# Two-layer decoder block on one core: the group pipeline of the first layer put in another order

## The chip, the core and the metric

The kernel runs on one core of a Trainium2 chip. The core has five engines that run their own instruction streams and meet at semaphores: TensorE (PE, with its weight loads PEld), VectorE (DVE), ScalarE (ACT), GpSimd (POOL) and SyncE (SP), which here only issues DMAs. The metric is the device time of one execution in microseconds (us).

## The reference, cut to what matters

A batch of 16 sequences of 100 tokens, 256 wide, goes through two decoder layers. Each is x + self-attention, then x + cross-attention to a context of 361 rows, then x + a mixture of experts. The change touches the first layer up to its experts. Cut to its core, this is:

```python
# A: attention over random features
h = layernorm(x)
q = tanh(h @ W_charge.T + b);  shell = h @ W_shell.T + b;  shell /= norm(shell)
proj = shell @ omega.T + rff_bias
phi_s = concat([cos(proj), sin(proj)]);  phi = (powers_of(q) x phi_s) @ W_combine.T
logits = phi @ phi.T * T / temp          # causal mask, softmax
x = x + (softmax(logits) @ V) @ W_out.T + b_out
# B: cross-attention
h = layernorm(x)
x = x + softmax(q(h) @ k(ctx).T) @ v(ctx)
# C: block with 16 causal heads of 16; D: router and experts
h = layernorm(x, ln1);   x1 = h + ...     # the normed x enters the sum
x = x + attention(h) @ wo + bo
scores = layernorm(x, ln2) @ gate_w      # top 2 of 8 experts, softmax over the two
```

## The kernel before, in words

The 16 sequences are four groups of four (`NB = 4`, `NG = 4`), and each group is two halves h of two sequences (200 tokens). In the first layer two kinds of work are laid side by side:

- `early(g, h)` takes half h of group g through A and B. It is one chain of small steps: norm (`norm_dve`), transpose (`turn_pe`, `turn_act`), the product `A_in` (L933), square and norm of the shell (L1901 to L1908), the angle (`A_omega`, L943, then six DVE instructions L1913 to L1923, named the angle chain here), the sine on ACT (L1440), the product `A_comb` (L947), nine DVE instructions L1930 to L1938 (the phi chain), the logits, softmax, values, `A_out`; then B with its own softmax. The last step of B adds to `x` and writes `xall`.
- `behind(g, routed)` takes the whole group g through C, the layer's attention with 16 heads (`attend`, 19 steps of which 16 make scores), and D, the router's scores. If `routed`, it also does the routing of the group before: `route` on DVE in two parts (ranking; then places, after `ahead`, L1026 to L1029, has counted tokens on PE), and eight indirect DMAs `send` on POOL.

`in_turn(early(0, 0), early(0, 1))` runs first, alone. Then `woven` is called for each group g from 0 to 2: it deals out `ROUNDS` rounds, in each one step of early(g+1, 0), one of behind(g), one of early(g+1, 1), one of behind(g). The yields of the generators are the steps; every engine has its own copy of them. The call for g = 0 stands alone, those for 1 and 2 are a loop (`Fori`). At the end behind(3) runs alone. What counts for the order: each engine does its instructions strictly in the order that this dealing gives, so an instruction that waits holds up everything dealt after it, on its engine, of both kinds of work.

In `attend`, step n makes scores n on PE (L1041, L1044) in one of two PSUM banks; DVE takes the maximum (L1995), subtracts (L1999); ACT takes the exponential (L1489); PE transposes (L1052), ACT copies (L1495), PE multiplies by the values (L1063); DVE sums (L2005). POOL builds `headbd` (L1708) for two steps ahead. `root_pool` (L466 ff.) does the inverse root of a norm on POOL.

The softmax quotient of A (L1954, L1956) and B (L1977, L1980) is multiplied into the exponentials before they are transposed.

## Time and profile before

| | us |
|---|---|
| median of three runs | 1689.74 (1689.53 to 1692.46) |
| the profiled execution's own time | 1689.45 |
| its span, first to last instruction | 1687.8 |
| PE busy / DVE / ACT / POOL | 1285.4 / 998.3 / 522.3 / 415.1 |

The span divides into: preparation to 20 us; early(0) alone from 21 to 92; the woven groups 0, 1 and 2 from 92 to 215, to 338 and to 464; behind(3) alone to 540; then the experts of the first layer and the whole second layer, which the change doesn't touch. "Idle before" in a row is the time in which the engine stood still ahead of that instruction, and the name behind the arrow is what ended it. The granted clock is the share of TensorE's full clock that it was given.

### The profile page before, as it was taken

How to read it: one execution, taken by the hardware profiler on the slowest of the kernel's cores; microseconds unless marked ns; L12 is line 12 of the kernel's file. 1: busy time of each engine (PE TensorE's matmuls, PEld its weight loads, DVE VectorE, ACT ScalarE, POOL GpSimd, SP SyncE). 2: the span in 40 equal slices, each digit the busy share in tenths (PEclk: the TensorE clock that was granted, in tenths of full speed). 3: DMA queues.
4: the chain of work that ended last, by engine and by line, in shares of the span. 5: the costliest groups of instructions: out<-in, count | busy, mean ns of one | idle time of the engine just before them, and what ended most of it. 6: DMA issues, size and time to landing. Idle time of an engine off the chain costs nothing.

```text
span 1687.8 us, 24678 instructions
## 1 busy us (share of the span) xinstructions
PE 1285.4 (76%) x7936; PEld 890.2 (53%) x7936; DVE 998.3 (59%) x2156; ACT 522.3 (31%) x1279; POOL 415.1 (25%) x528
## 2 busy tenths in 40 slices
PE   2677868767877699981458977779787697986987
PEld 1554654644644366651237754467554475644755
DVE  4447557457455233325676765768656686677852
ACT  2214324324322222210125512346213363233620
POOL 1032143243253200006622111311212212032100
PEclk9778878878888799995679989779897799987988
DMA  9510010191014211101315310044100350104501
GB/s 376 217 28 1 19 28 13 34 408 49 25 46 198 59 47 44 44 29 45 117 39 98 86 40 12 10 101 111 40 12 2 86 122 21 32 11 88 114 5 46
DMA packets 69693, 122.37 MB, mean 73 GB/s; under 512 B 25404, under 2 KB 55100, under 8 KB 68032
## 3 DMA queue, kind: packets, MB, share of 16 engines
q1 hardware_dynamic: 63936, 110.04, 21.7%
q0 software_dynamic: 5632, 10.77, 2.3%
q8 instruction: 66, 1.08, 0.3%
q14 instruction: 59, 0.48, 0.1%
HBM read 67.69 MB, written 53.07 MB: 72 GB/s over the span
## 4 chain that ended last, share of the span: by engine, by line
PE 46%; issue 24%; DVE 12%; POOL 8%; DVEq 3%; ACT 3%; DMA 2%; POOLq 2%; SPq 0%; ACTq 0%
PE ps L1143 7%; PE ps L1390 5%; PE ps L1162 3%; PE ps L525 3%; PE ps L1316 3%; PE ps L1332 3%; PE ps L533 2%; POOL experts L1779 2%; PE ps L1302 2%; PE ps L1403 2%; PE ps L933 1%; PE ps L1041 1%; POOL headbd L681 1%; PE ps L504 1%; DVE probs L1999 1%
## 5 line engine op out<-in xcount | busy, mean ns | idle before, releaser
L1628 ACT ACTIVATE probs<-ps,small 100x361 f32<-100x361 f32 x256 | 141.3, 557 | 94.1 <-DVE small L2347 89.5
L2347 DVE TENSOR_REDUCE small<-ps 100x2 f32<-100x722 f32 x128 | 115.7, 906 | 36.2 <-PE ps L1302 36.2
L1143 PE MATMUL ps<-every,xT_t 128*128 x256 | 122.3, 601 | 0.4 <-issue 0.4
L1390 PE MATMUL ps<-hT,experts 128*128 128x400 f32 x288 | 117.1, 558 | 1.2 <-DVE small L730 1.2
L1316 PE MATMUL ps<-cst,probs 100*121 100x100 f32 x768 | 104.0, 271 | 8.1 <-DVE probsT L2355 7.7
L1316 PEld LDWEIGHTS ps<-cst,probs 100*121 100x121 f32 x768 | 94.8, 185 | 22.2 <-issue 13.7
L2355 DVE TENSOR_SCALAR probsT<-ps 121x600 f32<-121x600 f32 x128 | 99.2, 775 | 9.1 <-PE ps L1316 9.1
L1332 PE MATMUL ps<-probsT,values_ 121*32 121x100 f32 x1536 | 90.8, 253 | 0.9 <-DVE probsT L2355 0.9
L1302 PE MATMUL ps<-k_stack,q_stack 96*100 96x362 f32 x256 | 81.8, 400 | 6.3 <-ACT probs L1628 5.6
L473 POOL TENSOR_TENSOR small<-small,cst 100x2 f32<-100x2 f32 x56 | 11.1, 198 | 295.3 <-DVE small L453 295.2
L1390 PEld LDWEIGHTS ps<-hT,experts 128*128 128x128 f32 x288 | 59.6, 215 | 42.2 <-issue 14.1
L681 POOL TENSOR_TENSOR headbd<-kT,cst 128x800 f32<-128x800 f32 x32 | 48.6, 1525 | 126.1 <-DVE kT L2237 95.7
L1192 PE MATMUL ps<-identb,xq 100*128 100x100 bf16 x128 | 13.4, 240 | 83.9 <-DVE y L2222 46.9
L504 PE MATMUL ps<-cst,xn 100*128 100x100 f32 x192 | 35.1, 328 | 52.3 <-DVE xn L459 34.7
L1403 PE MATMUL ps<-experts,probsT 128*100 128x256 f32 x288 | 70.2, 388 | 4.0 <-DVE probsT L2382 3.5
L594 PE MATMUL ps<-headbd,qT 128*100 128x400 f32 x128 | 60.1, 553 | 13.4 <-POOL headbd L681 13.4
L1332 PEld LDWEIGHTS ps<-probsT,values_ 121*32 121x32 f32 x1536 | 62.4, 109 | 13.9 <-DVE probsT L2355 1.8
L1708 POOL TENSOR_TENSOR headbd<-kT,cst 128x800 f32<-128x800 f32 x32 | 48.9, 1528 | 82.3 <-PE ps L1044 70.0
L1795 POOL TENSOR_TENSOR k_hi<-k_all,cst 128x362 fp32r<-128x362 f32 x32 | 26.4, 824 | 165.0 <-ACT k_all L1580 165.0
L1489 ACT ACTIVATE probs<-probs 100x400 f32<-100x400 f32 x64 | 34.3, 537 | 101.3 <-DVE probs L1999 101.2
L1995 DVE TENSOR_REDUCE small<-ps 100x4 f32<-100x400 f32 x64 | 36.5, 570 | 48.4 <-PE ps L1044 46.5
L1041 PE MATMUL ps<-headbd,qT 128*100 128x400 f32 x128 | 60.7, 558 | 3.2 <-ACT qT L1515 2.6
(329 smaller groups left out, 2887.2 us busy)
## 6 DMA issues: line engine op xcount, KB each, us to landing
k_stack<-key_d SPq DMA_DIRECT2D x192, 90.5 KB, 3.1
tok_d<-wt SPq DMA_DIRECT2D x1, 14848.0 KB, 45.5
res_d<-wt SPq DMA_DIRECT2D x1, 14848.0 KB, 42.0
every<-e_d SPq DMA_DIRECT2D x8, 1536.0 KB, 11.6
ctxT<-ctxT_d SPq DMA_DIRECT2D x8, 726.0 KB, 4.3
key_d<-k_hi SPq DMA_DIRECT2D x32, 181.0 KB, 2.8
key_d<-k_lo SPq DMA_DIRECT2D x32, 181.0 KB, 3.4
gates<-gate_d SPq DMA_DIRECT2D x28, 200.0 KB, 4.4
```

Source lines behind the costliest of these rows:

```text
L594: e.matmul(o, qT[:, c, b * S:(b + 1) * S], headbd[:, u % 2, 4 * i:4 * i + 4, :].rearrange("p h n -> p (h n)"), start=True, stop=False)
L681: inc(e.tensor_tensor(headbd[:, u % 2], keysT[:, c, b * S:(b + 1) * S].unsqueeze(1).broadcast_to([P, HC, S]), cs("head").unsqueeze(2).broa ...
L1041: e.matmul(o, qT[:, c, b * S:(b + 1) * S], headbd[:, m // 2 % 2, 4 * q:4 * q + 4, :].rearrange("p h n -> p (h n)"), start=True, stop=False)
L1143: ins = e.matmul(ps[:, 2 * i + t % 2, :], xT_t[:, t % 2, c, :], every[:, bass.ds(base + (i * DC + c) * HID0, HID0)], start=(c == 0), stop= ...
L1302: ins = e.matmul(bank(2 * (n % 2) + i, S, LE), q_stack[:, c * HC + h, b * S:(b + 1) * S], k_stack[c][:, h // 2, :], start=True, stop=True)
L1316: ins = e.transpose(ps[0:KW, 4 + i, k * S:(k + 1) * S], f_e[:, n % 2, i, k * KW:(k + 1) * KW], identS)
L1332: ins = e.matmul(ps[quarter(h), 6, (2 * (b % 2) + c) * S:(2 * (b % 2) + c + 1) * S], strip(3 * (b % 2) + k, KW, c, h), f_eT[:, n % 2, i, k ...
L1390: ins = e.matmul(bank(2 * i + j % 2, n=NT), w[:, c, :], hT[:, c, :], start=(c == 0), stop=(c == DC - 1))
L1403: ins = e.matmul(ps[0:S, 4 + b // 2, (b % 2) * D:(b % 2 + 1) * D], g_hid[:, (j - 1) % 2, b * S:(b + 1) * S], experts[:, o - D:o], start=(j ...
L1628: ins = e.activation(f_e[:, n % 2, i, 0:LC], bank(2 * (n % 2) + i, S, LC), ACT.Exp, bias=h_nm[:, n % 2, i:i + 1], accum_out=h_sum[:, b, h: ...
L2347: inc(e.tensor_reduce(h_nm[:, n % 2, 0:2], ps[0:S, 2 * (n % 2):2 * (n % 2) + 2, 0:LC], AX, ALU.max, negate=True), "F_nm")
L2355: inc(e.tensor_scalar(f_eT[:, n % 2], ps[0:KW, 4:6, 0:KC * S], 1.0, None, ALU.mult), "F_pT")
```

## The change: what it does

Six things, all in the first layer:

1. A's norm of group g+1 is drawn ahead: its statistics and its scaling are two steps (`norm_ahead`) dealt near the end of the group before, behind B's `B_qbk` and `B_nm` steps on DVE, its roots on POOL likewise. `early` begins with the transpose on PE. Since nothing else then orders them, PE's `A_in` waits for a new signal `B_x`, set by the last step of B.
2. Both parts of `route` and the PE part `ahead` move: part one to behind the scaling of C's norm, part two and `ahead` into attention step 0. PE waits for the places at step 3 rather than at C's second projection. POOL's eight sends go to steps 7, 9, 11, 13, 14, 15, 16 and 17.
3. Empty steps are set behind long chains (after the angle chain, after `A_out`, after B's softmax, and at places in `behind`): `ROUNDS` goes from 18 to 20.
4. One sine instruction for both halves, which waits for the second half's angles.
5. The quotients of A's and B's softmax are left off the exponentials, and the token's reciprocal is multiplied in by the instruction that adds the result to `x` (two `scalar_tensor_tensor` of 100x256 in place of one `tensor_tensor` of 100x512).
6. The loop over groups 1 and 2 is written out.

```diff
-ROUNDS, STEPS = 18, 19
+ROUNDS, STEPS = 20, 19
+SEND_AT = {7: 0, 9: 1, 11: 2, 13: 3, 14: 4, 15: 5, 16: 6, 17: 7}
...
             def early(g, h):                                    # PE
-                yield
                 turn_pe(e, "A_", g, h, "hTp", p, xnX, ("A_xn", 1))
                 yield
                 W(e, "A_hT", g, 1, h)
+                if g:
+                    W(e, "B_x", g - 1, 1, h)
...
                 for n in range(STEPS):                          # PE, attend
                     if n < 16:
                         scores(n)
+                    if routed and n == 0:
+                        ahead(g - 1)
                     if 2 <= n <= 17:
                         turn(n - 2)
+                    if routed and n == 3:
+                        e.wait_ge(r_placed.sem, r_placed.at(g - 1))
...
             in_turn(early(0, 0), early(0, 1))
-            woven(early(1, 0), early(1, 1), behind(0, False))
-            with e.Fori(1, NG - 1) as g:
-                woven(early(g + 1, 0), early(g + 1, 1), behind(g, True))
+            for g in range(NG - 1):
+                woven(early(g + 1, 0), early(g + 1, 1), behind(g, g > 0))
             list(behind(NG - 1, True))
...
-                W(e, "A_ang", g, 1, h)                          # ACT
-                inc(e.activation(a_trig[:, t], a_ang[:, t], ACT.Sin), "A_trig")
+                yield
+                if h == 0:
+                    W(e, "A_ang", g, 1, 1)
+                    e.activation(a_trig, a_ang, ACT.Sin).then_inc(names["A_trig"].sem, 2)
...
+            def norm_ahead(g, h):                               # DVE
+                e.wait_ge(ld["x"].sem, g * 16 + 16)
+                inc((yield from norm_dve(e, "A_", g, h, xin, xnX)), "A_xn")
+                yield
+
             def early(g, h):
                 p, q, t, o = 2 * h, 2 * h + 1, tok(h), own(h)
-
-                if h == 0:
-                    e.wait_ge(ld["x"].sem, g * 16 + 16)
-                inc((yield from norm_dve(e, "A_", g, h, xin, xnX)), "A_xn")
+                norm = norm_ahead(g + 1, h) if g + 1 < NG else iter(())
...
-                W(e, "A_e", g, 1, h)
-                e.reciprocal(a_rs[:, o], a_sum[:, o])
-                e.drain()
-                inc(e.tensor_tensor(lg, lg, a_rs[:, o].unsqueeze(2).broadcast_to([S, HB, S]), ALU.mult), "A_p")
                 yield
                 yield
                 W(e, "A_out", g, 1, h)
                 W(e, "A_xb", g, 1, h)
-                add_out(x, p, h)
+                e.reciprocal(a_rs[:, o], a_sum[:, o])
+                e.drain()
+                for i, b in enumerate(seqs(h)):
+                    e.scalar_tensor_tensor(x[:, b, :], ps[0:S, p, i * D:(i + 1) * D], a_rs[:, b:b + 1], x[:, b, :],
+                                           ALU.mult, ALU.add)
...
                 inc(e.tensor_scalar(b_qbk[:, o], bank(p, S, HB), 1.0, None, ALU.mult), "B_qbk")
+                next(norm, None)
                 yield
...
                 for h in range(2):                              # DVE, behind
                     list(norms[h])
                     e.drain()
                     for b in seqs(h):
                         ins = e.tensor_scalar(xn[:, b, :], y[:, b, :], r2Y[:, b:b + 1], None, ALU.mult)
                     inc(ins, "C_xn")
-                    if h == 0:
-                        next(ways, None)
-                    yield
+                    yield
+                next(ways, None)
+                yield
```

Three places in the order. First DVE, ahead of the attention of groups 1 and 2, before the change: `L1995` and `L1999` are the first attention step's maximum and difference, `L1913` to `L1923` the first half's angle chain.

```order
L1908 TENSOR_TENSOR values_<-values_,small 100x2x64 x2
L426 ISA
L1995 TENSOR_REDUCE small<-ps 100x4
L1999 TENSOR_TENSOR probs<-ps,small 100x400
L1913 TENSOR_SCALAR values_<-ps,wt 64x200
L1915 TENSOR_SCALAR values_<-values_ 64x200
L1917 TENSOR_SCALAR values_<-values_ 64x200
L1919 SCALAR_TENSOR_TENSOR values_<-values_ 64x200
L1921 SCALAR_TENSOR_TENSOR values_<-values_ 64x200
L1923 TENSOR_SCALAR values_<-values_ 64x200
```

The same place after it (lines are shifted: `L1929` to `L1939` is the second half's angle chain, `L2017` and `L2021` the maximum and difference, `L2061` the copy of C's values out of PSUM):

```order
L2061 TENSOR_SCALAR xn<-ps 100x512
L1929 TENSOR_SCALAR values_<-ps,wt 64x200
L1931 TENSOR_SCALAR values_<-values_ 64x200
L1933 TENSOR_SCALAR values_<-values_ 64x200
L1935 SCALAR_TENSOR_TENSOR values_<-values_ 64x200
L1937 SCALAR_TENSOR_TENSOR values_<-values_ 64x200
L1939 TENSOR_SCALAR values_<-values_ 64x200
L2017 TENSOR_REDUCE small<-ps 100x4
L2021 TENSOR_TENSOR probs<-ps,small 100x400
```

Both angle chains now stand ahead of the attention's first step instead of behind its first and second.

What stands on DVE behind that first step in groups 1 and 2 after the change (`L2104` to `L2118` is the routing's second part, `L2110` its wait for PE's count, `L1947` the start of the phi chain):

```order
L2017 TENSOR_REDUCE small<-ps 100x4
L2021 TENSOR_TENSOR probs<-ps,small 100x400
L2104 TENSOR_TENSOR small<-small 100x32
L2106 TENSOR_REDUCE small<-small 100x4
L2108 TENSOR_TENSOR small<-small 100x4
L2110 TENSOR_TENSOR small<-small,ps 100x64
L2113 TENSOR_REDUCE small<-small 100x8
L2114 TENSOR_REDUCE small<-small 100x8
L2116 CAST place_all<-small 100x8
L2117 CAST place_now<-small 100x8
L2118 TENSOR_TENSOR small<-small 100x8
L1947 TENSOR_SCALAR values_<-ps 100x2x64
```

The routing's second part has moved from ahead of C's projections to between the first attention step and the first phi chain.

Then PE, late in the attention of group 0, before: `L533` is the second `A_out` product, `L1041` with `L1044` are scores, `L1052` a transpose, `L1063` values, `L504` the transpose of B's first normed half.

```order
L1052 MATMUL ps<-cst,probs 100x100 x4
L1063 MATMUL ps<-probsT,values_ 32x100 x4
L533 MATMUL ps<-wt,experts 100x256 x4
L1041 MATMUL ps<-headbd,qT 100x400
L1044 MATMUL ps<-causalb,identb 100x400
L1052 MATMUL ps<-cst,probs 100x100 x4
L1063 MATMUL ps<-probsT,values_ 32x100 x4
L504 MATMUL ps<-cst,experts 128x100 x4
L1041 MATMUL ps<-headbd,qT 100x400
```

After (`L1046` and `L1049` scores, `L1057` transpose, `L1068` values, `L505` the transpose of B's first half; the row above the first is the scores product that belongs to it, and the second `A_out` product is directly before that):

```order
L1049 MATMUL ps<-causalb,identb 100x400
L1057 MATMUL ps<-cst,probs 100x100 x4
L1068 MATMUL ps<-probsT,values_ 32x100 x4
L1046 MATMUL ps<-headbd,qT 100x400
L1049 MATMUL ps<-causalb,identb 100x400
L1057 MATMUL ps<-cst,probs 100x100 x4
L1068 MATMUL ps<-probsT,values_ 32x100 x4
L1046 MATMUL ps<-headbd,qT 100x400
L1049 MATMUL ps<-causalb,identb 100x400
L1057 MATMUL ps<-cst,probs 100x100 x4
L1068 MATMUL ps<-probsT,values_ 32x100 x4
L505 MATMUL ps<-cst,experts 128x100 x4
```

Between the second `A_out` and B's first transpose there now stand three whole attention steps instead of one.

## Rows read from the trace of the kernel before

**Rows 1.** Windows by stage; columns: us, busy us (instructions) per engine, granted clock, DMA share

```profile
91.60:214.70 123.10, 91.59 (x533) 63.63 (x532) 73.87 (x180) 41.25 (x96) 34.71 (x46) 0.85 0.06 16
214.70:338.10 123.40, 93.41 (x542) 64.83 (x542) 75.61 (x199) 41.24 (x96) 43.50 (x54) 0.83 0.08 24
...
214.70:247.60 32.90, 20.47 (x94) 16.09 (x94) 19.04 (x60) 5.66 (x14) 15.52 (x25) 0.74 0.08 22
247.60:267.50 19.90, 15.02 (x55) 7.29 (x55) 15.89 (x41) 8.85 (x13) 6.45 (x6) 0.69 0.04 12
267.50:302.80 35.30, 28.45 (x212) 17.97 (x209) 24.81 (x57) 14.66 (x38) 14.50 (x16) 0.98 0.04 12
...
464.10:488.20 24.10, 14.64 (x67) 12.55 (x67) 10.91 (x38) 3.86 (x8) 9.70 (x17) 0.72 0.18 67
```

**Rows 2.** Timeline of PE, opening of a group: start us, us, form [idle before <-releaser]

```profile
220.91 1.15 PE L1029 MATMUL ps<-small,cst 100*100 100x24 f32 x6
...
231.94 3.72 PE L933 MATMUL ps<-wt,experts 128*100 128x321 f32 x8
...
238.58 2.33 PE L933 MATMUL ps<-wt,experts 128*100 128x321 f32 x8
...
247.68 0.91 PE L1041 MATMUL ps<-headbd,qT 128*100 128x400 f32 x2 [0.61 <-ACT qT L1515]
```

**Rows 3.** Timeline of DVE, same group, opening and first attention steps

```profile
217.56 0.19 DVE L2072 TENSOR_REDUCE small<-small 100x4 f32<-100x32 f32 x1
...
220.08 0.26 DVE L2076 TENSOR_SCALAR small<-small 100x32 f32<-100x32 f32 x2
...
230.55 0.61 DVE L2032 TENSOR_SCALAR xn<-y,small 100x256 f32<-100x256 f32 x2
...
250.48 1.55 DVE L1915 TENSOR_SCALAR values_<-values_ 64x200 f32<-64x200 f32 x1
...
255.69 0.26 DVE L1915 TENSOR_SCALAR values_<-values_ 64x200 f32<-64x200 f32 x1
...
259.00 0.28 DVE L1930 TENSOR_SCALAR values_<-ps 100x128 f32<-100x128 f32 x1
...
261.91 0.29 DVE L1938 TENSOR_TENSOR values_<-values_,ps 100x128 f32<-100x128 f32 x1
```

**Rows 4.** Timeline of POOL, same group

```profile
222.82 0.20 POOL L473 TENSOR_TENSOR small<-small,cst 100x2 f32<-100x2 f32 x1 [0.23 <-DVE small L453]
...
225.33 0.71 POOL L484 TENSOR_TENSOR small<-small,cst 100x2 f32<-100x2 f32 x1
...
250.39 1.52 POOL L1708 TENSOR_TENSOR headbd<-kT,cst 128x800 f32<-128x800 f32 x1 [1.63 <-PE ps L1044]
```

**Rows 5.** Timeline of ACT, same group, around the sines

```profile
254.05 1.28 ACT L1489 ACT_TABLE_LOAD   x1
255.34 0.54 ACT L1489 ACTIVATE probs<-probs 100x400 f32<-100x400 f32 x1
```

**Rows 6.** Timeline of PE, same group, middle and end

```profile
280.19 0.38 PE L964 MATMUL ps<-cst,values_ 100*100 100x100 f32 x2 [2.09 <-DVE values_ L1956]
...
283.72 0.38 PE L964 MATMUL ps<-cst,values_ 100*100 100x100 f32 x2 [1.50 <-DVE values_ L1956]
...
301.37 0.56 PE L504 MATMUL ps<-cst,experts 100*128 100x100 f32 x4 [2.69 <-DVE experts L459]
...
326.31 3.17 PE L533 MATMUL ps<-wt,qT 128*100 128x256 f32 x8 [1.99 <-DVE qT L2048]
```

**Rows 7.** Timeline of DVE, same group, end

```profile
331.95 0.74 DVE L459 TENSOR_SCALAR bdx<-y,small 100x256 f32<-100x256 f32 x2 [0.27 <-issue]
```

**Rows 8.** DVE by line and form: count | busy us, mean ns | idle before

```profile
L2296 DVE SCALAR_TENSOR_TENSOR x<-ps,small,xall 100x256 f32<-100x256 f32 x16 | 7.0, 478 | 2.7 <-PE ps L533 1.8 <-issue 0.8
...
L1986 DVE TENSOR_TENSOR xall<-ps,x 100x512 f32<-100x512 f32 x4 | 2.8, 692 | 11.2 <-PE ps L1017 11.2
```

**Rows 9.** Timeline of PE, front of the first group, nothing beside it

```profile
40.13 4.71 PE L947 MATMUL ps<-wt,values_ 64*100 64x320 f32 x8 [2.11 <-ACT values_ L1440]
```

More of the change, by code:

```diff
@@ L1525, in behind @@
                     yield
[L1526 to L1527 removed]
+                for _ in range(3):
+                    yield
             in_turn(early(0, 0), early(0, 1))
[L1530 to L1531 removed]
+            for g in range(NG - 1):
                 woven(early(g + 1, 0), early(g + 1, 1), behind(g))
@@ L1691, in early @@
                 inc(e.tensor_tensor(a_rn[:, own(h)], a_ss[:, own(h)], cs("mhalf", S)[:, 0:HB], ALU.pow), "A_rn")
+                e.wait_ge(ld["rows"].sem, 16)
+                inc(add_bias(x, xin, "A_out", h), "A_xb")
                 yield
-                for _ in range(7):
+                for _ in range(8):
                     yield
```

121 lines of the change are left out of this document (65 added, 56 removed).

## Prediction, on record before the changed kernel was run

> **What bounds the kernel now.** I read the windows by stage first, because the share of busy time over the whole span mixes stages. Groups 0 and 1 of the woven part take 123.10 and 123.40 us, and in them PE, the busiest engine, works 91.6 and 93.4 us, DVE 73.9 and 75.6 [rows 1]. So no engine is the bound: some 30 us of each group is PE standing still in a chain that goes from engine to engine, and PE's own work sets a floor that no reordering passes, about 30 us below each group's time, 90 in all. The same view cuts group 1 into stretches. In its opening (32.90 us, up to the first attention scores) PE works 20.47 and its granted clock is 0.74; in the second stretch (19.90) DVE works 15.89 and PE 15.02 at 0.69; in the middle (35.30) PE works 28.45 at 0.98 [rows 1]. The idle time is in the opening above all, then in the other two. Next the timelines, which tell what PE waits for. In the opening, which starts at 214.7, the first `A_in` product starts only at 231.94 and the second at 238.58 [rows 2]; ahead of them DVE had A's norm, C's norm and both parts of the routing to do, and gave the last of these, C's scaled second half, at 230.55 [rows 3]. In the middle and at the end PE's waits name the softmax quotients (2.09 and 1.50), the norm of B (2.69) and C's copy of its attention (1.99) [rows 6].
>
> **The sum is made for three woven groups, the prologue and the last group.** I walked the new order by hand, each instruction starting when its operands are there and its engine is free, with durations of the rows (where no group stands behind a duration it is a sum of short rows of the same timelines, read in group 1); T is the end of the last product of the group before (214.7 in group 1).
>
> *Opening.* Before, 32.90 us [rows 1]. After: A's norm has been drawn ahead, so `turn_pe`, the copies and the first `A_in` (3.72 us, [rows 2]) stand at T and need only `B_x`, the addition that DVE makes at about T + 1. DVE then goes on with C's statistics (two halves of 1.1 us, to T + 3.5); POOL's root of them takes 3.2 us from its first row to the end of its last [rows 4], in two halves to T + 5.7 and T + 8.9; DVE makes the shell's chain (1.9) and C's norm and scaling (1.45) up to about T + 12.1. Then the cost of the move: part one of the route, from 217.56 to 220.3, that is 2.8 us [rows 3], stands between the first half's shell and the second's. The second shell is there at T + 15.6, and since PE does its instructions in order, its transpose `A_shTp` holds up what is dealt behind it of C's projections: 10.1 us of them remain (3.1 + 3.1 + 2.9 of products and two transposes of 0.5), to T + 25.9, and ACT's copy and the start of the scores make T + 27.3. That is 5.6 us less in groups 1 and 2. Group 0 has no route: 25.2 where its own opening takes 31.8, 6.6 less.
>
> *Second stretch.* Both angle chains (L1913 to L1923, 2.2 us each without neighbours) now come before the attention's first step and lie beside PE's projections. One sine for two means two table loads fewer of four, 1.28 us each [rows 5]; ACT isn't the bound there, but the first exponentials stand behind them. Against this, `ahead` (six products of L1029, the group 1.15, and what is ahead of them, some 2.0 in all) and part two of the route (nine instructions, 1.65) now lie in the stretch, between the first attention step and the phi chain (L1930 to L1938, 3.2 us, [rows 3]). The walk gives 17.6 for 19.90, 2.3 less; without the route (group 0) 5.5 less.
>
> One row speaks against a gain here: the angle chain's L1915 takes 1.55 us at 250.48 beside POOL's L1708, which runs from 250.39 to 251.91, and 0.26 at 255.69 with POOL idle [rows 3, 4]. Moved into the opening, the chains meet POOL's first two `headbd` instructions; I count one such block of 1.3 us per group, and the bounds are none and two, 4 us either way over three groups. The Trainium skill, SBUF — State Buffer, "Who interferes with whom", says that DVE and GpSimd share a port pair under an exclusive lock; the two rows agree with it, and without the lock the sum would be about 4 us lower.
>
> *ACT's tables.* By the rows a load takes 1.28 us and the exponential starts 1.29 after the load's start [rows 5]: two loads save 2.6 us of ACT per group. The Trainium skill, ScalarE: Activation LUTs, "What ACT_TABLE_LOAD costs", adds a drain of some 1380 ns to each; by that two loads would be 5.3 us, and the sum up to 8 us lower. The rows don't show the drain, and the sum goes by them.
>
> *Middle.* The walk of the new order needs 30.1 us for what takes 35.30 now. The waits it loses are PE's two on the quotient (2.09 + 1.50) and the one on B's norm (2.69) [rows 6], since the transposes wait for the exponentials alone and three attention steps stand between the second `A_out` and B's first transpose where one did. One `tensor_tensor` of 692 ns becomes two `scalar_tensor_tensor` of 478 ns [rows 8], 0.26 us more per half, on DVE and not on PE. I take 5.0 per group. If DVE is late with the norm all the same, the wait moves to the next transposes and perhaps half comes.
>
> *End.* The two quotients of B leave the path, and its scores of both halves stand back to back. Norm-ahead adds 3.7 us of DVE (statistics 2 x 1.1, scaling 2 x 0.74 as the L459 row, [rows 7]), in time in which DVE waits for PE. D's norm starts at 326.6 instead of 331.95 [rows 7], with it PE's wait of 1.99 at 326.31 [rows 6], and the last product ends 3.8 earlier. With DVE's 3.7 uncovered it would be nothing.
>
> *Outside.* In the prologue one sine waits for the second half's angles and its table load: the first `A_comb` at 40.13 [rows 9] moves to 43.8, 3.6 later, and the quotients give 1.8 back: + 2 (bounds 0 and + 4). The last group's opening, 24.10 [rows 1], goes to 22.5, but `ahead` and the route's second part now lie in its attention without work beside them: + 1. POOL's last four sends come at every step, and the loads of the next `xin` are issued long before they are read: nothing. Writing out the loop I count at nothing: the straight group 0 and the looped group 1 take 123.10 and 123.40 [rows 1], so between - 0.6 and + 3 for code fetched fresh. The experts and layer two only shift.
>
> Sum: groups 1 and 2 give 5.6 + 2.3 + 5.0 + 3.8 = 16.7 each, group 0 6.6 + 5.5 + 5.0 + 3.8 = 20.9, together 54.3; less 3 outside: 51. The profiled execution takes 1689.45, its span 1687.8 plus 1.65 around it, and the median of the runs is 1689.74, the same within 0.3. So 1638.
>
> **Rivals.** *Half of it.* Waits on DVE and in PE's order take the place of those removed. For it: DVE is at 15.89 of 19.90 in the second stretch [rows 1], PE stands behind `A_shTp` in the opening, and a hand walk always finds less idle time than a chip. Against: the largest term, the norm's 17 us ahead of the first `A_in`, leaves no queue that it could wait in. The opening's and the middle's gain halved, the second stretch nothing, the end whole: 2.8 + 2.5 + 3.8 = 9.1 in groups 1 and 2, 3.3 + 2.5 + 3.8 = 9.6 in group 0, less the 3 outside gives - 25, about 1664; with the end halved too, 1670.
>
> *More, by the clock.* The granted clock is 0.74 in the opening and 0.69 in the second stretch, with PE idle for a third and a quarter of them, and 0.98 in the middle, where it is seldom idle [rows 1]. 20.47 + 15.02 us of PE at those clocks would be about 25.9 us at 0.98: if filling the gaps raises the clock, PE's part shrinks, and with half of these 9.6 on the path each group gains some 5 more: about 1622. Against it: the opening still has short products with gaps behind every copy.
>
> *Slower.* The new order serializes at the attention's first step: the opening stays at 32.9, because the route's part and both angle chains now stand on DVE ahead of the step's maximum, and the second stretch becomes one chain, the blocks of POOL and DVE included: angle 4.7, blocks 5.2, tables and sine 3.1, `ahead` 2.2, route 1.7, phi chains 6.6, four shifts 6.8, that is 30.3 where 19.90 were. That is 10.4 lost against 8.8 kept in the middle and at the end: + 1.6 in three groups, and + 3 outside, about 1697. It decides from the point at which DVE's second angle chain ends later than the first scores by more than 9 us. Against it: the shell's second half is there at T + 15.6 in the walk, 12 before the scores.
>
> *The change doesn't do it.* If `B_x` or the `x` load held `A_in` back as the norm did, the opening would keep its 32.90 and the time would be near 1654; this lies inside the second case.
>
> **Numbers.** The forecast 0.62, half 0.24, more 0.10, slower 0.04. 1638 is the likeliest; the forecast's own terms (one block more or less 4, prologue 2, middle 2 to 3 per group, loop 3) give about 1625 to 1652. From 1620 to 1670 the range holds most of the first three cases and leaves 2 in 10 out. A difference below 0.2% (3.4 us) can't be told from none here. Faster 0.94, the same 0.02, slower 0.04.
>
> **What would show it.** In the profile after: group 0 near 102 us and group 1 near 107; PE's first `A_in` within 5 us of T; the opening near 27; no wait of PE's transposes on a quotient; D's norm about 112 us after T; prologue's first `A_comb` near 44. It would be wrong if DVE's idle time ahead of the first shift has vanished and PE waits there for DVE, if L1915 and the chain beside it take 1.5 us more than once in most groups, if the route's first part delays C's transposes by more than its 2.8 us, or if the clock in the opening leaves 0.7 for 0.9.

## The result, and the profile after

The changed kernel takes 1674.29 us (median of 7 runs, 1667.32 to 1699.75), the kernel before in the same session 1692.46 (7 runs, 1687.58 to 1695.92). The ratio is 0.989 with a 95% interval of 0.986 to 0.993: faster by 18 us, or 1.1%, where 51 were forecast and 1670 was the upper end of the range. The run of 1699.75 was a slow one (granted clock 0.839 where the others have 0.848 to 0.861) and is left out of the ratio. The profiled execution has a span of 1665.6 us for 1687.8, that is 22.2 less; it is the fastest of the seven, and the stages below are those of this pair of executions. They are cut at T (the last product of a group), at the first attention scores (s0), the fifth (s4) and the sixteenth (s15) of a group, the same events in both traces. The forecast's "second stretch" ended some 3 us behind s4; its gain is compared with the stretch s0 to s4. The stages moved by - 21.1 us together; the remaining 1.1 lie behind them, where the change does nothing.

| | before | after | moved | forecast |
|---|---|---|---|---|
| prologue, to T at | 91.6 | 94.4 | + 2.8 | + 2 |
| opening T to s0, groups 0 / 1 / 2 | 31.9 / 33.0 / 34.6 | 26.3 / 31.0 / 30.0 | - 5.6 / - 2.0 / - 4.7 | - 6.6 / - 5.6 / - 5.6 |
| s0 to s4 | 17.7 / 16.6 / 17.8 | 19.0 / 19.1 / 17.6 | + 1.3 / + 2.5 / - 0.2 | - 5.5 / - 2.3 / - 2.3 |
| middle s4 to s15 | 37.4 / 37.5 / 37.3 | 34.9 / 35.8 / 35.5 | - 2.5 / - 1.7 / - 1.9 | - 5.0 each |
| end s15 to T | 36.2 / 36.3 / 36.3 | 32.8 / 32.4 / 30.0 | - 3.4 / - 4.0 / - 6.3 | - 3.8 each |
| last group, T to the experts' first product | 101.3 | 106.0 | + 4.6 | + 1 |

Group 1 in the view of windows (columns as in [rows 1]), opening, s0 to s4, middle, end; [rows 1] has before's:

```profile
207.30:238.27 30.97, 20.69 (x90) 15.37 (x88) 21.57 (x49) 5.73 (x14) 14.20 (x22) 0.78 0.09 24
238.27:257.37 19.10, 13.10 (x50) 7.11 (x51) 15.40 (x42) 6.25 (x10) 3.61 (x3) 0.72 0.01 2
257.37:293.15 35.78, 30.96 (x216) 19.37 (x215) 27.30 (x58) 13.85 (x36) 17.54 (x18) 0.88 0.05 13
293.15:325.50 32.35, 27.85 (x195) 22.58 (x194) 16.74 (x48) 12.58 (x33) 7.76 (x13) 0.92 0.18 50
```

PE's own work in the group is 92.6 us (the sum of its column) where it was 93.4. So of the 5.2 us that the group is shorter 4.4 are idle time, and 25.6 us of the 30.0 are left.

PE in the opening and behind it, against [rows 2]:

```profile
208.26 4.57 PE L935 MATMUL ps<-wt,experts 128*100 128x321 f32 x16 [0.25 <-ACT experts L519]
...
223.89 0.60 PE L941 MATMUL ps<-cst,values_ 100*128 100x100 f32 x2 [3.60 <-DVE values_ L1924]
224.28 3.62 PE L534 MATMUL ps<-wt,hT 128*100 128x256 f32 x8
227.69 2.55 PE L526 MATMUL ps<-hT,wt 128*128 128x200 f32 x8
...
238.27 0.89 PE L1046 MATMUL ps<-headbd,qT 128*100 128x400 f32 x2 [0.80 <-POOL headbd L1718]
...
241.78 1.32 PE L950 MATMUL ps<-wt,values_ 64*100 64x320 f32 x4 [1.65 <-ACT values_ L1448]
...
255.36 0.88 PE L1057 MATMUL ps<-cst,probs 100*100 100x100 f32 x4 [4.35 <-ACT probsT L1505]
```

The first `A_in` product starts 1 us behind T (207.3), 16 earlier in the group than before, as forecast. But the second shell's transpose waits until 223.89 (T + 16.6), and the projections behind it run at half clock: L534's eight products take 3.62 us here and 1.97 at 230.71. The first scores come at T + 31.0 and not T + 27.3. Behind them PE stands still ahead of `A_comb` (1.65, for the sine) and 4.35 us ahead of the second attention transpose.

DVE in the same time, against [rows 3]:

```profile
216.66 2.12 DVE L2054 TENSOR_SCALAR xn<-y,small 100x256 f32<-100x256 f32 x2
...
219.50 1.31 DVE L749 TENSOR_TENSOR small<-small 100x256 f32<-100x256 f32 x1
220.89 1.16 DVE L751 TENSOR_TENSOR small<-small,cst 100x256 f32<-100x256 f32 x1
...
223.54 0.29 DVE L1924 TENSOR_TENSOR values_<-values_,small 100x128 f32<-100x128 f32 x1
...
236.37 1.99 DVE L1933 TENSOR_SCALAR values_<-values_ 64x200 f32<-64x200 f32 x1
...
243.13 0.29 DVE L1947 TENSOR_SCALAR values_<-ps 100x128 f32<-100x128 f32 x1 [0.67 <-PE ps L950]
...
247.39 0.57 DVE L2017 TENSOR_REDUCE small<-ps 100x4 f32<-100x400 f32 x1
...
252.83 0.29 DVE L1955 TENSOR_TENSOR values_<-values_,ps 100x128 f32<-100x128 f32 x1
253.04 0.57 DVE L2017 TENSOR_REDUCE small<-ps 100x4 f32<-100x400 f32 x1
```

L2054 (0.63 at 213.59), L749 and L751 (0.42 alone) and L1933 (0.26 alone) are stretched beside POOL's bias additions (L1684) and its `headbd` (L1718):

```profile
216.26 1.27 POOL L1684 TENSOR_TENSOR x<-xin,rows 100x512 f32<-100x512 f32 x1
217.48 1.14 POOL L1684 TENSOR_TENSOR y<-y,rows 100x512 f32<-100x512 f32 x1
...
220.50 1.27 POOL L1684 TENSOR_TENSOR y<-y,rows 100x512 f32<-100x512 f32 x1
...
236.73 1.52 POOL L1718 TENSOR_TENSOR headbd<-kT,cst 128x800 f32<-128x800 f32 x1
```

From 243.13 to 247.4 and from 249.0 to 253.1 DVE does the two phi chains, each ahead of a maximum (L2017) whose scores PE had made at 244.6 and 248.9. ACT waits for that:

```profile
239.89 1.28 ACT L1448 ACT_TABLE_LOAD   x1 [1.88 <-DVE values_ L1939]
241.19 0.54 ACT L1448 ACTIVATE values_<-values_ 64x400 f32<-64x400 f32 x1
...
243.04 0.54 ACT L1499 ACTIVATE probs<-probs 100x400 f32<-100x400 f32 x1
248.64 0.54 ACT L1499 ACTIVATE probs<-probs 100x400 f32<-100x400 f32 x1 [5.07 <-DVE probs L2021]
254.29 0.54 ACT L1499 ACTIVATE probs<-probs 100x400 f32<-100x400 f32 x1 [5.11 <-DVE probs L2021]
254.73 0.49 ACT L1505 ACTIVATE probsT<-ps 100x400 f32<-100x400 f32 x1
```

The table load for the one sine stands behind the wait for the second angle chain (1.88 us of waiting, then 1.28 of load). In the kernel before it ran ahead of that wait: the load started at 250.61, right behind an exponential, and the sine waited another 1.76 us after it (253.66). So the change also laid a load of 1.28 us open, which neither the text of the change nor the prediction says; why the load takes the other place is not known. The third exponential waits 5.11 us for DVE, and the copy of the first transposed probabilities (254.73), which PE had made by 249.6, stands behind it on ACT. PE's 4.35 us come from this chain of waits.

In the middle, against [rows 6]:

```profile
286.49 0.52 PE L1057 MATMUL ps<-cst,probs 100*100 100x100 f32 x4 [1.96 <-ACT probsT L1505]
...
290.81 0.88 PE L1057 MATMUL ps<-cst,probs 100*100 100x100 f32 x4 [1.76 <-ACT probsT L1505]
...
297.27 0.52 PE L1057 MATMUL ps<-cst,probs 100*100 100x100 f32 x4 [1.06 <-ACT probs L1499]
...
309.48 3.78 PE L534 MATMUL ps<-wt,qT 128*100 128x256 f32 x16 [0.78 <-DVE qT L2071]
```

No transpose waits for a quotient or for B's norm any more. But PE now waits 1.96, 1.76 and 1.06 us for the attention's own chain, and its clock is 0.88 where the middle had 0.94 (the window before, cut at the same events).

In the stretch s0 to s4 of groups 0, 1 and 2 the granted clock is 0.68, 0.72 and 0.71, where it was 0.85, 0.73 and 0.84. PE is busy for 13.8, 13.1 and 13.8 us in it, where it was for 10.8, 11.8 and 10.9 (`ahead` adds about 1 in groups 1 and 2), so PE's idle time there fell by 3.6 us over the three groups while its busy time grew by 7.2.

### The profile page after: what moved, and what is told of

It is laid out like the page before. It is cut to its first block, busy times and chain, and to the rows that moved or that the text cites. A ratio compares the mean times of both kernels' runs of the same rounds, so it can differ in the third digit from the quotient of the medians.

```text
span 1665.6 us, 24431 instructions
## 1 busy us (share of the span) xinstructions
PE 1284.8 (77%) x7936; PEld 886.7 (53%) x7936; DVE 1008.3 (61%) x2148; ACT 513.7 (31%) x1269; POOL 413.2 (25%) x528
## 4 chain that ended last, share of the span: by engine, by line
PE 39%; issue 31%; DVE 10%; POOL 9%; POOLq 3%; DVEq 3%; ACT 2%; DMA 2%; SPq 1%; another core or an unknown queue 0%; ACTq 0%
PE ps L1150 7%; PE ps L1169 3%; PE ps L1323 3%; PE ps L1397 3%; PE ps L1339 3%; PE ps L526 2%; POOL experts L1792 2%; PE ps L1309 2%; PE ps L534 2%; POOL headbd L682 2%; PE ps L1068 1%; PE ps L1046 1%; PE ps L595 1%; PE ps L1410 1%; PE ps L1057 1%
## 5 line engine op out<-in xcount | busy, mean ns | idle before, releaser
L2372 DVE TENSOR_REDUCE small<-ps 100x2 f32<-100x722 f32 x128 | 115.7, 907 | 37.5 <-PE ps L1309 37.3
L474 POOL TENSOR_TENSOR small<-small,cst 100x2 f32<-100x2 f32 x56 | 10.9, 195 | 282.1 <-DVE small L454 282.0
L1718 POOL TENSOR_TENSOR headbd<-kT,cst 128x800 f32<-128x800 f32 x32 | 48.9, 1529 | 120.3 <-PE ps L1049 78.2
L505 PE MATMUL ps<-cst,xn 100*128 100x100 f32 x192 | 34.4, 324 | 54.4 <-DVE xn L460 34.8
L1046 PE MATMUL ps<-headbd,qT 128*100 128x400 f32 x128 | 68.4, 622 | 6.4 <-POOL headbd L1718 2.4
L1499 ACT ACTIVATE probs<-probs 100x400 f32<-100x400 f32 x64 | 34.4, 537 | 121.3 <-DVE probs L2021 114.0
L595 PE MATMUL ps<-headbd,qT 128*100 128x400 f32 x128 | 60.3, 551 | 13.8 <-POOL headbd L682 12.0
L1808 POOL TENSOR_TENSOR k_hi<-k_all,cst 128x362 fp32r<-128x362 f32 x32 | 26.3, 822 | 167.6 <-ACT k_all L1590 167.6
L1570 ACT ACTIVATE xqT<-ps 128x400 bf16<-128x400 bf16 x32 | 16.1, 504 | 157.6 <-PE ps L1215 90.9
```

What stands on the lines that cost most here:

```text
L595: e.matmul(o, qT[:, c, b * S:(b + 1) * S], headbd[:, u % 2, 4 * i:4 * i + 4, :].rearrange("p h n -> p (h n)"), start=True, stop=False)
L1046: e.matmul(o, qT[:, c, b * S:(b + 1) * S], headbd[:, m // 2 % 2, 4 * q:4 * q + 4, :].rearrange("p h n -> p (h n)"), start=True, stop=False)
L2372: inc(e.tensor_reduce(h_nm[:, n % 2, 0:2], ps[0:S, 2 * (n % 2):2 * (n % 2) + 2, 0:LC], AX, ALU.max, negate=True), "F_nm")
```

## The experiments

Fifteen runs were made, the first of them of the changed kernel once more. The runs of one kernel lie 10 to 30 us apart and go with the granted clock (below); so beside each median stand the stages of its one profiled execution. Ratios are to the kernel before. "Faster" and "slower" compare with the changed kernel, 1674 and (first experiment) 1677 us. It did not run again beside the later ones, but the kernel before did, at medians of 1689.5 to 1691.1, so the sessions agree within 3 us. Against this scatter a difference below some 5 us in a median isn't settled.

**The changed kernel again.**

> The changed kernel once more, for its own scatter and a second profile. Theory: its group 1 (about 118 us, 5 more than group 2) repeats, since it comes from the order and not from chance; total 1667 to 1680, ratio to before 0.987 to 0.992. Rival: the groups change places from one execution to the next, and the total lies elsewhere in 1665 to 1700.

1677.29 us (6 runs), ratio 0.992 (0.989 to 0.995). Groups 0 to 2 take 118.8, 119.7 and 114.0 us where they took 112.9, 118.2 and 112.9. The openings and s0 to s15 agree within 1.5 us; the end of group 0 is 38.8 for 32.8 with the same waits, at a mean clock of 0.76 for 0.89. Group 1 being the longest repeats; a single end of a group says nothing below 6 us. The three ends take 38.8, 35.6 and 29.9 us here, 104.3 for 108.8 before the change, a gain of 4.5 us where the first profile has 13.7.

**The loop written out, in the kernel before.**

```diff
-            with e.Fori(1, NG - 1) as g:
+            for g in range(1, NG - 1):
```

> The kernel before with its loop over groups 1 and 2 written out, nothing else. Theory: no difference that can be told (within 3 us), as I counted it. Rival: code that is fetched fresh costs 3 to 8 us and makes the times scatter more (the changed kernel's lie 15 us apart in the fast state, those of before 8).

1690.25 (12 runs), ratio 0.999 (0.996 to 1.002). The median doesn't move: writing the loop out costs nothing that can be told, as counted. The times scatter more (1678.6 to 1705.0; before 1685.8 to 1701.9), as the rival says, with no cost in it.

**Quotients back in the changed kernel.**

```diff
+                W(e, "A_e", g, 1, h)                # one step behind A_nm; B alike
+                e.reciprocal(a_rs[:, o], a_sum[:, o])
+                inc(e.tensor_tensor(lg, lg, a_rs[:, o]..., ALU.mult), "A_p")
...
-                    e.scalar_tensor_tensor(x[:, b, :], ps[...], a_rs[:, b:b + 1], x[:, b, :], ...)
+                add_out(x, p, h)
```

> The changed kernel with the quotients of both softmaxes multiplied into the exponentials again and the plain addition at the end of A and B; the rest stays. Theory: in the woven part the waits of PE on the quotient come back (some 1.5 to 2 us at each of A's two transposes) and B's end gets longer, but part of them only takes the place of PE's waits on the attention's own chain: 2 to 3 us a group and 2 in the prologue, 7 to 11 us slower than the changed kernel. Rival (as I forecast: the waits come back in full): 4 to 5 us a group, 15 or more slower.

1689.89 (12 runs), ratio 0.999 (0.997 to 1.001): 13 to 16 us slower than the changed kernel, between the theory and the rival and nearer the rival. Without this edit the other five together bring nothing. The waits on the quotient are back in group 1 (1.63 and 1.49 us). But not all of the loss is waiting: the ends take 40.1, 38.7 and 37.4 us for 32.8, 32.4 and 30.0, with PE busy 33.2 to 35.5 us at a clock of 0.72 to 0.77, for 26.6 to 29.0 at 0.89 to 0.96.

**The quotients alone, in the kernel before.**

> The kernel before with one of the six edits alone: the quotients of both softmaxes are multiplied in by the instruction that adds to x. Theory (putting them back into the changed kernel cost 13 to 16 us, so nearly the whole gain is theirs, and the other five edits cancel): 12 to 17 us faster than before, ratio 0.990 to 0.993. Rival (they pay only where PE has attention steps to do instead, which the empty steps provide): less than 8 us faster.

1682.76 (12 runs), ratio 0.993 (0.989 to 0.997). That is 7 us, half of what they are worth in the new order. The middle gets shorter by 1.5 to 1.9 in each group (35.8, 35.9, 35.4), the waits of 2.09 and 1.50 gone; its end does not (36.4, 36.4, 34.8 where 35.5, 35.7, 35.6 were, both cut where L1017 ends). So the theory's 12 to 17 falls, and the rival's "less than 8" holds: the quotients bring more together with the other edits. How much of the difference is the clock, these runs don't tell.

**A's norm at the head of its group again.**

```diff
-                norm = norm_ahead(g + 1, h) if g + 1 < NG else iter(())
-                yield
+                norm = iter(())
+                e.wait_ge(ld["x"].sem, g * 16 + 16)
+                inc((yield from norm_dve(e, "A_", g, h, xin, xnX)), "A_xn")
+                yield
...
                 inc(e.tensor_scalar(ang, ang, 3.1415925, ...), "A_ang")
                 yield
-                yield
```

> The changed kernel with A's norm at the head of its group again, in the first two steps as before; one of the two empty steps, the one behind the angle chain, makes room for it, the rest of the order stays. Theory (drawing the norm ahead shortens the opening by some 3 to 5 us a group and gives back 2 to 4 at the end of the group, where its 3.7 us of DVE stand ahead of B's softmax and D): 0 to 6 us slower than the changed kernel in all, opening 3 to 5 longer, end 2 to 3 shorter. Rival (as I forecast, the cover at the end is whole): 12 us or more slower.

1684.06 (12 runs), ratio 0.994 (0.991 to 0.997): 7 to 10 us slower than the changed kernel, between the two. The place wasn't what was expected: the openings of groups 1 and 2 stay (30.8, 30.3; group 0 has 28.3 for 26.3), and s0 to s4 grows to 21.2, 22.1 and 22.1, since the second shell comes later against C's projections and the first `A_comb` then waits 4.74 us for the sine:

```profile
240.44 0.92 PE L1046 MATMUL ps<-headbd,qT 128*100 128x400 f32 x2
...
247.07 2.45 PE L950 MATMUL ps<-wt,values_ 64*100 64x320 f32 x4 [4.74 <-ACT values_ L1448]
...
260.53 0.88 PE L1057 MATMUL ps<-cst,probs 100*100 100x100 f32 x4 [2.97 <-ACT probsT L1505]
```

So in groups 1 and 2 norm-ahead did not shorten the opening, though the first `A_in` starts 9 us earlier with it (T + 1.0 for T + 10.1 in group 1); it let A's chain be further on when the attention began. The edit also takes out an empty step, and the two are not told apart.

**The empty step behind A_out moved behind B's scores.**

```diff
                 proj_pe(e, h, wv("A_out", DC), qTX, p, "A_out")
                 yield
-                yield
...
                 inc(ins, "B_s")
                 yield
                 yield
+                yield
```

> The changed kernel with the empty step behind A_out taken out on every engine and set behind B's scores, so that one attention step instead of three stands between the second A_out and B's first transpose. Theory (three attention steps in a row are a chain of their own through DVE and ACT and leave PE waiting 1.96 + 1.76 us, so the wait for B's norm was only exchanged): the middle of each group moves by less than 1.5 us, the total by less than 4, either way. Rival (as I forecast: the step buys B's norm its time): PE waits 2 to 3 us for the norm again, 2 to 4 us a group, 6 to 12 slower.

1681.57 (12 runs), ratio 0.993 (0.990 to 0.997): 4 to 7 slower. The middle is 40.7, 41.4 and 42.1, some 6 us longer, and the end 29.9, 29.6 and 27.3, some 3 shorter. PE waits 5.11 us for B's norm:

```profile
283.29 0.52 PE L1057 MATMUL ps<-cst,probs 100*100 100x100 f32 x4 [0.33 <-ACT probsT L1505]
...
289.39 0.93 PE L505 MATMUL ps<-cst,experts 100*128 100x100 f32 x4 [5.11 <-DVE experts L460]
...
294.42 0.93 PE L505 MATMUL ps<-cst,experts 100*128 100x100 f32 x4 [0.96 <-DVE experts L460]
```

My theory here falls, and the forecast's own reading holds: the three attention steps do buy B's norm its time, and cost less (1.96 + 1.76) than they save.

**A sine for each half.**

```diff
-                if h == 0:
-                    W(e, "A_ang", g, 1, 1)
-                    e.activation(a_trig, a_ang, ACT.Sin).then_inc(names["A_trig"].sem, 2)
+                W(e, "A_ang", g, 1, h)
+                inc(e.activation(a_trig[:, t], a_ang[:, t], ACT.Sin), "A_trig")
```

> The changed kernel with one sine for each half, as before, at the same places of the order. Theory (the join and the table load behind its wait are on the path): the first A_comb of the prologue comes about 3.6 earlier, in each group the first A_comb about 2 us and the first exponential about 1 us earlier, table loads stay two per group; 6 to 9 us faster than the changed kernel in all. Rival (ACT's table loads are what counts, the join is hidden behind DVE): no gain in the groups, at most 3.6 from the prologue.

1668.53 (6 runs), ratio 0.985 (0.982 to 0.988): 6 to 9 faster. The prologue's `A_comb` starts at 41.40, against 44.48 in the changed kernel and 45.26 in its repetition, and the groups still have two table loads, now one in front of the first sine and one in front of the exponential. But in the groups s0 to s4 is 17.5, 18.6 and 18.6, no shorter: PE's wait ahead of `A_comb` is gone, and it waits 1.75 us for the phi chain instead. Its table load starts without a wait (233.68), so the load that the one sine laid open is hidden again, and the groups are no shorter for it. The rival holds for the groups; the gain that is shown is the prologue's.

**The route's first part one step later.**

```diff
-                next(ways, None)
                 yield
+                next(ways, None)
                 for h in range(2):
                     W(e, "C_vp", g, 1, h)
```

> The changed kernel with part one of the route one step later on DVE, in front of the copy of C's first values, where DVE stands idle 4.1 us. Theory (the route in front of the second shell holds up PE's in-order queue): the second A_shTp comes about 4.3 us earlier in groups 1 and 2, the first scores 3 to 4 earlier, 6 to 9 us faster in all. Rival (the time is given back at the attention's first step, where DVE and the sine decide): the scores start earlier and the total moves by less than 3.

1667.27 (6 runs), ratio 0.983 (0.978 to 0.987): 7 to 10 faster. The openings of groups 1 and 2 are 27.7 and 26.5 for 31.0 and 30.0, and the walk's 27.3 is met. The theory holds for the openings, 6.8 us together.

**The attention one step earlier.**

```diff
                     projT_pe(e, h, wv("C_q", DC), hT, 5 + 2 * h, "C_qTp")
                 yield
-                yield
                 yield from attend(g, routed)
+                yield
```

> The changed kernel with the attention of each group begun one step earlier (an empty step ahead of it set behind it), so that DVE makes the first two maximum and difference pairs ahead of the first phi chain, and only then the two phi chains. Theory (in the second stretch DVE's in-order phi chains hold up PE's transposes, which wait 2.7 to 4.35 us): first scores to fifth 3 to 4 us shorter, 6 to 10 us faster in all. Rival (DVE is the bound there, or PE at half clock): the wait moves to the phi transposes and the total moves by less than 3.

1668.96 (6 runs), ratio 0.986 (0.983 to 0.989): 5 to 8 faster. s0 to s4 is 13.3, 15.6 and 15.5, 2 to 6 shorter, and the ends are 37.4, 37.4 and 36.5, longer, at a clock of 0.77 in group 1.

```profile
248.02 0.88 PE L1057 MATMUL ps<-cst,probs 100*100 100x100 f32 x4 [5.16 <-ACT probsT L1505]
```

DVE is at the third maximum 11.3 us behind s0 (245.70 for 234.41) where it needed 14.8 (253.04 for 238.27), with one phi chain ahead of it and not two, and almost no idle time in either. PE's wait ahead of the second transpose has not shrunk (5.16 for 4.35): PE has less to do before it, at a clock of 0.85 for 0.72. So the theory holds in its stage, by DVE's order; the wait that it named only ends earlier.

**The last group's route in its opening.** The placing of before the change for that group alone.

> The changed kernel with the last group's route and count back in its opening, as before the change; groups 1 and 2 keep the new places. Theory (the last group has nothing to hide them under): its attention from first to last scores goes from 35.2 back to about 31, its opening stays at 23.5 or grows by less than 1; 3 to 4 us faster in all. Rival: the opening grows by as much, no gain.

1678.22 (8 runs), ratio 0.993 (0.989 to 0.997). The last group's scores take 31.0 us from first to sixteenth for 35.4, the opening 24.1 for 23.7, the group 103.5 for 106.0 and 105.1. The stage does what the theory says; in the whole time 2 us can't be seen.

**POOL's bias additions out of the opening.**

```diff
-                e.wait_ge(ld["rows"].sem, 16)
-                inc(add_bias(x, xin, "A_out", h), "A_xb")
                 yield
-                for _ in range(8):
+                for _ in range(5):
                     yield
+                e.wait_ge(ld["rows"].sem, 16)
+                inc(add_bias(x, xin, "A_out", h), "A_xb")
+                for _ in range(3):
+                    yield
...
+                    if n in (13, 15):                    # in attend; C_xb
+                        inc(add_bias(y, y, "C_o", n // 15), "C_xb")
```

> The changed kernel with POOL's two kinds of bias additions (A's x and C's y, 100x512, four in each opening) moved out of the opening into the attention. Theory (beside them DVE's L2054 takes 2.12 us for 0.6 and two of the route's instructions 1.3 and 1.2 for 0.4, on the path to the second shell): the opening of groups 1 and 2 is 2.5 to 3.5 us shorter, some of it given back where they meet other work of DVE; 3 to 7 us faster in all. Rival: the blocks only move into the attention, where DVE is as tight; within 2 us.

1663.13 (6 runs), ratio 0.981 (0.976 to 0.986): 11 to 14 faster, more than expected. The openings are 25.3, 27.7 and 28.9, 5.4 us less together; where the rest comes from isn't shown. The DVE rows that were stretched are short:

```profile
213.13 0.61 DVE L2056 TENSOR_SCALAR xn<-y,small 100x256 f32<-100x256 f32 x2
...
214.47 0.42 DVE L749 TENSOR_TENSOR small<-small 100x256 f32<-100x256 f32 x1
214.96 0.43 DVE L751 TENSOR_TENSOR small<-small,cst 100x256 f32<-100x256 f32 x1
...
216.88 0.29 DVE L1926 TENSOR_TENSOR values_<-values_,small 100x128 f32<-100x128 f32 x1
```

L2056 takes 0.61 for 2.12, L749 and L751 0.42 and 0.43 for 1.31 and 1.16, and the second shell starts 13.1 us behind T (203.8) and not 16.2. That is the price of POOL's additions on DVE, 3.1 us in this opening; group 1's is 3.0 to 3.3 shorter, those of groups 0 and 2 by 1 to 1.6.

**The corrections together** (a sine per half in the prologue alone, the route's part later, the attention earlier, the last group's route in its opening).

> The changed kernel with what the other runs point to: separate sines in the prologue alone, the route's first part one step later, the attention one step earlier, the last group's route back in its opening. Theory, by adding up (4 + 7 + 6 + 1 us): 1657 to 1662. Rival (the terms share one wait, DVE's and ACT's at the attention's first step): not below 1665.

1638.04 (6 runs, 1635.32 to 1645.20), ratio 0.967 (0.963 to 0.972). This beats both kernels, by 52 and 36 us, and by more than the single ones add up to (the prologue's 4, then 7 to 10, 5 to 8 and 0). Group 1, same four stages:

```profile
200.30:227.81 27.51, 20.89 (x90) 15.27 (x88) 21.22 (x49) 5.73 (x14) 13.90 (x22) 0.81 0.06 15
227.81:243.40 15.59, 9.71 (x48) 5.47 (x49) 13.30 (x38) 5.11 (x7) 3.69 (x3) 0.84 0.01 2
243.40:276.30 32.90, 28.87 (x213) 17.74 (x211) 25.60 (x60) 13.96 (x37) 15.41 (x16) 0.97 0.05 13
276.30:307.60 31.30, 27.27 (x200) 21.78 (x199) 18.48 (x52) 13.45 (x35) 9.87 (x15) 0.95 0.19 53
```

Its opening is 27.5, s0 to s4 15.6, and middle and end run at 0.97 and 0.95: PE's busy time is 86.7 us, where the same instructions took 92.6 in the changed kernel. So the floor that the prediction set by PE's own work isn't fixed: the same instructions take less at the higher clock.

**Two of the four; three of the four; four and POOL's biases.** Three runs to tell apart what the combination consists of. The first is the route's part and the attention's begin:

> The changed kernel with two of the four corrections: the route's first part one step later and the attention one step earlier. Theory (the two waits lie one behind the other on the same path, so their gains add or more): 12 to 20 us faster than the changed kernel, about 1658. Rival (they need the others): not below 1664.

> The combination of corrections without the attention's earlier begin: separate sines in the prologue, the route's first part later, the last group's route in its opening. Theory: the second stretch is back at 17.5 to 19 us and the middle at 35.5 in groups 1 and 2, so some 14 to 20 us slower than the full combination (1638), at 1652 to 1658. Rival (the attention's place mattered only by 5 to 8 us, as it did alone): 1643 to 1647.

> The full combination and POOL's bias additions out of the opening as well. Theory (they block DVE in the opening, 2 to 3 us a group, whatever stands around them): 5 to 10 us faster than 1638, about 1630. Rival (with the route's part out of that place the blocks meet nothing that is waited for): within 3 us of 1638.

Two of the four give 1645.63 (6 runs), ratio 0.977 (0.972 to 0.981), 29 to 32 of the 36 to 39 us and far more than the theory's 12 to 20. Against it the full combination's profile has 4.0 us less in the prologue and 3.3 less in the last group up to its last product, as the two remaining corrections should give, the same stages within 0.1 us behind the openings of groups 1 and 2, and 4.0 more in group 0. Without the early attention the combination is at 1658.9 (6 runs), 0.981 (0.977 to 0.985), 21 slower than with it, about what the theory said; s0 to s4 takes 18.1, 17.5 and 19.0 again. With the biases moved as well the median of all six is 1654.3, but one run took 5509.88 and the other five have 1648.9 (ratio 0.980, 0.975 to 0.985): 11 slower, and both the theory and the rival fall. Group 1 of that one:

```profile
195.70:220.60 24.90, 19.72 (x88) 14.69 (x87) 18.34 (x49) 5.61 (x14) 9.55 (x18) 0.86 0.05 13
220.60:236.60 16.00, 9.74 (x49) 5.51 (x50) 13.71 (x38) 5.10 (x7) 4.78 (x4) 0.85 0.01 2
236.60:273.00 36.40, 32.74 (x214) 20.27 (x212) 25.90 (x59) 14.05 (x37) 16.50 (x17) 0.83 0.07 20
273.00:310.30 37.30, 33.54 (x199) 26.99 (x198) 18.42 (x52) 13.54 (x35) 11.99 (x17) 0.77 0.24 68
```

The opening is shorter by 2.6, as expected. Middle and end are longer by 3.5 and 6.0, and PE is busy for 32.74 and 33.54 us in them, against 28.87 and 27.27, with the same number of instructions within 1, at 0.83 and 0.77 for 0.97 and 0.95.

## Why the prediction was wrong

**The prologue and the end: right in this pair, in part by luck.** + 2.8 for + 2; the ends gave 13.7 us together where 11.4 were forecast. But a single end moves by up to 6 us with the clock, and in the changed kernel's second profile the three gave 4.5. The change also moved POOL's copies of the attention's reciprocals from behind the attention into its steps 12 and 18, which the list of six leaves out; no run takes that back alone.

**The opening: the order right, two sizes off.** The walk had the second shell at T + 15.6, and it came at T + 16.5. The block of POOL on DVE, which I counted once at 1.3 us, is 3.1 us in front of it. Another 2.9 lie in the second angle chain (L1931 1.13, L1933 1.99, then 0.62, for 0.26, 0.26 and 0.36), which delays not the first scores but the sine and the maximum behind them, and 2.1 in the two phi chains. The projections behind the second shell, 10.1 us by rows at full clock, took 13.2 (224.28 to 237.47): PE had been idle from 214.8 to 223.9 but for two short groups of transposes, and came back at half clock. 12.3 us came of 17.8.

**The step that failed is the second stretch.** The prediction took "2.3 less" and "5.5 less" from a walk that let the angle chains leave DVE and gave no weight to what then stands ahead of the attention's second and third maximum: the phi chains, 4.1 to 4.3 us each with a block in it, in group 1. Before the change the two angle chains stood there (3.7 and 2.3 us) and the phi chains came ahead of the fourth and fifth maximum. Measured, the stretch gave + 3.6 for the - 10.1 forecast, the largest miss of the table (13.7 of 29 us). The run with the attention one step earlier shows it: with one phi chain less ahead of the third maximum the three stretches take 44.4 us together, 7.7 less than before the change where 10.1 were forecast. In the corrected order that edit is worth 21 us in all, but by the profiles only 10 of them lie in this stretch; the rest is in the middle and the end, at a higher clock. In groups 0 and 2 the stretch's own clock also fell (0.85 to 0.68 and 0.84 to 0.71), which made PE's work there 3 us longer each. How much of that DVE's chain hides is not separated; in group 1, where DVE works from 234.61 to 253.68 with 0.67 us of idle time, nearly all.

**The middle: half the term.** The waits named went (2.09 and 1.50 on quotients, 2.69 and another 1.62 on B's norm). In their place stand 1.96, 1.76 and 1.06 us on the attention's own chain, and a clock of 0.88. 6.1 us came of 15. I had left the new wait out of the walk: the rival "half of it" had the mechanism, with too small a loss.

**The last group** lost 4.6 us and not 1: without work beside them, `ahead`, the route's nine instructions and the later first steps lie open, and the run that moved them back regained 4.4 in the attention (of which 1.6 to 2.5 reach the group's whole time).

**Of the rivals** the half case came nearest (1664 to 1670) and was still 4 to 10 us too fast. The clock as a rival was put only on the fast side; in the changed kernel it was no better than before (mean 0.861 for 0.857), with what group 1 gained in the opening and the end lost in the middle, and groups 0 and 2 lower from s0 to s4. By the rows of group 1 POOL's blocks come to some 8 us of DVE where the sum counted one of 1.3. The Trainium skill, SBUF — State Buffer, "Who interferes with whom", has one of the two engines wait for the other's whole instruction. The trace agrees: beside two additions of POOL two DVE instructions of 0.6 us together took 2.12, and moving the additions took them back to 0.61. The Trainium skill, ScalarE: Activation LUTs, "What ACT_TABLE_LOAD costs", puts a drain of some 1380 ns behind a table load; it doesn't show in the trace after either: the sine starts 1.30 us behind the load's start and the exponential likewise.

**The signs.** Two of those named for being wrong came: DVE's idle time ahead of the first shift, 4.93 us before, is gone in groups 0 and 1, and the blocks in group 1's second angle chain come to 2.9 us. The sign "D's norm about 112 us after T" can't stand beside a group of 107: it was taken from the old group with only its end changed. In the trace D's first scaling starts at T + 109.1 of 118.2. Two prices of rivals are also 1 to 2 us off in their own sums (1656 for 1654, 1623 for 1622), which changes nothing.

**What stays open.** Why the combination's clock stays near full is not settled. Its order differs from the one with POOL's biases moved only on POOL, and DVE's idle gaps and PE's waits in s0 to s4 are nearly the same (5.15 and 5.52 us, then 0.87 and 0.84); after the first of these waits (ended at 241.41 and 234.58) PE was back at full clock some 4 us later in the one and some 14 in the other. That the corrections bring 36 us together and some 20 singly goes with this: with the attention earlier alone PE is busy 66.2 us in the middle and end of group 1, and with the route's part later as well 56.1, with the same order behind the opening. The mean clock of the combination is 0.869 to 0.872 in all six runs, where the changed kernel has 0.848 to 0.861 in all but the one of 1699.75, so it isn't the luck of one execution; but why the one order keeps the clock and the other doesn't, no run here shows.

## What to carry to other kernels

When chains are moved out of a stretch, walk the in-order queue for what now stands ahead of the next instruction that the busiest engine waits for, since the moved chain's successor is likely to take its place. Test edits by pairs: each of two corrections gave 5 to 10 us alone and 29 together, and the quotients gave 7 in one order and 13 to 16 in the other; and look whether the surplus is waiting or clock. Where a long wait of PE remains, price what follows it at the lower clock as well.

## What the runs showed of the hardware

The granted clock is a cost of its own. With PE's order unchanged a middle of 32.9 us became 36.4 and an end of 31.3 became 37.3, PE being busy 28.9 and 27.3 us in the one and 32.7 and 33.5 in the other; it is on the 2.4 GHz level (1.0) or on the 1.2 one (0.5), and the length of the low time behind the same wait differs from one execution of the same kernel to the next (at the end of group 0, behind a wait of 2.93 us, some 4 us in one and some 16 in the other; the end takes 32.8 and 38.8 us). Two POOL additions over 100x512 beside a pair of DVE instructions stretched the pair from 0.6 to 2.1 us. A table load of 1.28 us ran ahead of the wait of the sine that needs it in the kernel before (250.61, the sine at 253.66) and behind that wait in the changed one (239.89, after 1.88 us): whether it is hidden has to be read from the trace.
